# Layer 0 of a four-layer graph network on one core: reciprocal degrees spread through memory, and degrees moved forward in two engines' orders

## The reference, cut to what matters

```python
H = (adj != 0);  w = adj.reshape(N, -1)[:, :C]        # first row of adj: edge weights
Dn = 1 / einsum('nce,ne->nc', H, w)                   # reciprocal degree of a node (0 where not positive)
Be = 1 / H.sum(axis=1)                                # reciprocal count of an edge
conv(x) = Dn * H @ (Be * (H^T @ (x @ W^T))) + b
h = layer_norm(relu(conv(x, W1, b1)));  y = conv(h, W2, b2) + x
x = layer_norm(x + y)
```

## Time and profile before

| | us |
|---|---|
| median of three runs | 668.26 (666.8 to 669.39) |
| the profiled execution | 670.04 |
| its span | 668.2 |
| TensorE busy | 623.1 (93%) |
| VectorE busy | 560.8 (84%) |
| ScalarE busy | 526.6 (79%) |
| GpSimd busy | 376.5 (56%) |

### The profile page before, as it was taken

One profiled execution on the slowest core, in us unless ns is written; L12 is line 12 of the kernel. 1 busy time (PEld: TensorE's weight loads), 2 busy tenths in 40 slices (PEclk: granted clock), 3 DMA queues, 4 the chain that ended last, 5 costly groups with the idle time before them and its releaser, 6 DMA issues.

```text
span 668.2 us, 15857 instructions
## 1 busy us (share of the span) xinstructions
PE 623.1 (93%) x5014; PEld 452.0 (68%) x5014; DVE 560.8 (84%) x1712; ACT 526.6 (79%) x1191; POOL 376.5 (56%) x448
## 2 busy tenths in 40 slices
PE   5989999999999999898999979999999997999993
PEld 4667777777777776565666646666666664778882
DVE  3889998888888888778999888988988987688886
ACT  4667888877777777868999788787877785899995
POOL 1234556665555557756777435353535353899983
PEclk9999999999999999998999999999999998999998
DMA  9591338354646433344655334545453443487773
GB/s 271 182 233 48 80 65 221 79 145 82 149 87 150 86 65 63 63 81 89 103 110 98 63 75 85 111 81 109 83 110 83 103 87 64 81 188 188 180 188 127
DMA packets 174466, 76.14 MB, mean 114 GB/s; under 512 B 122160, under 2 KB 173872, under 8 KB 174384
## 3 DMA queue, kind: packets, MB, share of 16 engines
q1 hardware_dynamic: 164208, 66.34, 42.3%
q0 software_dynamic: 8448, 8.39, 8.5%
q10 hardware_dynamic: 1728, 0.40, 0.3%
HBM read 28.97 MB, written 8.39 MB: 56 GB/s over the span
## 4 chain that ended last, share of the span: by engine, by line
PE 30%; DVE 8%; POOL 6%; DMA 6%; ACT 3%; issue 2%; SPq 0%; ACTq 0%; POOLq 0%; DVEq 0%
PE banks L86 9%; PE banks L88 8%; PE banks L87 8%; DMA xT_lo<-x_halves 3%; DMA l_TT_lo<-l_T_lo 3%; DVE l_st L1057 2%; POOL x_halves L1143 2%; POOL l_rstd L1082 2%; PE banks L1237 2%; POOL l_U L2048 1%; PE banks L1605 1%; POOL l_T_lo L1845 1%; ACT l_t L1658 1%; DVE l_u L1762 1%; DVE l_rsum L1768 1%
## 5 line engine op out<-in xcount | busy, mean ns | idle before, releaser
L1091 ACT ACTIVATE x_resident<-l_pre,l_nmr,l_rstd 128x256 f32<-128x256 f32 x256 | 140.8, 605 | 7.7 <-POOL l_nmr L1085 7.7
L983 POOL TENSOR_TENSOR hq<-hq 128x512 f32<-128x512 f32 x48 | 71.7, 1493 | 90.9 <-ACT hq L690 88.6
L1143 POOL TENSOR_TENSOR x_halves<-x_resident,x_halves 128x1024 f16<-128x1024 f32 x46 | 98.1, 2133 | 16.5 <-DVE l_pre L1339 9.9
L1057 DVE BATCH_NORM_STATS2 l_st<-l_pre 128x6 f32<-128x256 f32 x256 | 93.3, 410 | 0.0
L86 PE MATMUL banks<-Wk_lo,xT_hi 128*128 128x512 f16 (+1 forms) x256 | 83.4, 326 | 3.3 <-DVE l_pre L1339 1.8
L87 PE MATMUL banks<-Wk_hi,xT_lo 128*128 128x512 f16 (+1 forms) x256 | 83.3, 325 | 0.0
L88 PE MATMUL banks<-Wk_hi,xT_hi 128*128 128x512 f16 (+1 forms) x256 | 83.2, 325 | 0.0
L1082 POOL TENSOR_TENSOR l_rstd<-l_veps,minus_half 128x4 f32<-128x4 f32 x64 | 71.7, 1121 | 15.1 <-DVE l_veps L1071 11.2
L86 PE MATMUL banks<-W2T_lo,h_hi 128*128 128x257 f16 x256 | 70.2, 274 | 3.5 <-DVE h_lo L849 1.3
L88 PE MATMUL banks<-W2T_hi,h_hi 128*128 128x257 f16 x256 | 70.1, 274 | 0.0
L87 PE MATMUL banks<-W2T_hi,h_lo 128*128 128x257 f16 x256 | 70.1, 274 | 0.0
(11 more groups left out here) (200 smaller groups left out, 1904.8 us busy)
## 6 DMA issues: line engine op xcount, KB each, us to landing
adj<-in_adj SPq DMA_DIRECT2D x32, 256.0 KB, 3.5
x_halves<-in_x SPq DMA_DIRECT2D x16, 512.0 KB, 4.3
x_resident<-b_half SPq DMA_DIRECT2D x8, 1024.0 KB, 7.9
x_resident<-in_x POOLq DMA_DIRECT2D x16, 512.0 KB, 5.9
out<-x_resident SPq DMA_DIRECT2D x15, 512.0 KB, 3.2
x_resident<-in_L_gnn_W SPq DMA_DIRECT2D x2, 512.0 KB, 5.5
x_resident<-in_L_gnn_Wk SPq DMA_DIRECT2D x1, 768.0 KB, 9.6
xT_hi<-x_halves SPq DMA_TRANSPOSE x48, 3.2
```

The lines of the kernel that those rows point to most:

```text
L983: pool.tensor_tensor(hq[:, 0, :], hq[:, 0, :], hq[:, h, :], ALU.add).then_inc(hqs_ok, 1)
L1057: dve.bn_stats(L.st[p][:, j, :], L.pre[p][:, j, :]).then_inc(L.st_ok, 1)
L1091: act.activation(K.x[:, gcols(g, j)], L.pre[p][:, j, :], ACT.Identity, bias=L.nmr[p][:, j:j + 1], scale=L.rstd[p][:, j:j + 1]).then_inc(L. ...
L1143: pool.tensor_tensor(F.xs[p][1], x_group(K, g), F.xs[p][0], ALU.subtract).then_inc(F.x_lo, 1)
```

## The change

For groups 6 to 15 (`BY_ROWS = 6`) the spreading by TensorE and the copy by ScalarE are left out. SyncE writes `dinv` to a row of 2 KB in memory, waits until it has landed, and reads the row back, broadcast to 128 partitions, into `dbc`; the elements lie there in the order (node, graph), so `operator` reads `dbc` with a step of four. These two DMAs stand at the head of SyncE's step g, ahead of the loads of group g + 2. VectorE's two casts go, and `degrees` of the next group waits until the write has landed. For all groups from 2 on, TensorE's `degree` stands right behind `mix_x` and not behind `project(g-1, 2)`, and VectorE's `degrees` stands ahead of both `mixed_low`.

```diff
+BY_ROWS = 6
+        K.rows = nc.dram_tensor("degree_rows", (G, N, GP), F32)
@@ sync
+        def spread_degrees(g):
+            sp.wait_ge(dchain, upto(g, 4, 4))
+            sp.dma_start(K.rows[g], dinv[:]).then_inc(row_out, 16)
+            sp.wait_ge(row_out, 16 * (g - BY_ROWS) + 16)
+            sp.wait_ge(pf_ok, upto(g - 1, 1, 1))
+            sp.dma_start(dbc[:], K.rows[g:g + 1].rearrange("a n j -> a (n j)").to_broadcast([128, C])).then_inc(
+                dbc_in, 16)
@@ sync step
+            if has(0) and g >= BY_ROWS:
+                spread_degrees(g)
             if has(2):
                 load(g + 2, p)
@@ tensor: transpose_adj
-            if reused(g, 1):
+            if g > BY_ROWS:
+                pe.wait_ge(dchain, upto(g - 1, 4, 2))
+            elif g > 0:
                 pe.wait_ge(dbc_sb, upto(g - 1, 1, 1))
@@ tensor step
-            if has(0):
+            if has(0) and g < BY_ROWS:
                 spread_degrees(g, p)
...
                 mix_x(g, p, 1)
+            if has(1) and g > 0:
+                degree(g + 1, q)
             once(g, 0, W.fold, pe)
             if has(-1):
                 project(g - 1, 2)
-            if has(1):
+            if has(1) and g <= 0:
                 degree(g + 1, q)
@@ scalar step
-            if has(1):
+            if has(1) and g < BY_ROWS - 1:
                 copy_degrees(g + 1)
@@ vector: degrees
+            if g > BY_ROWS:
+                dve.wait_ge(row_out, 16 * (g - BY_ROWS))
             dve.tensor_tensor(dinv[:], drc[:], dpos[:], ALU.mult).then_inc(dchain, 1)
+            if g >= BY_ROWS:
+                return
@@ vector: operator
+            if g >= BY_ROWS:
+                dve.wait_ge(dbc_in, 16 * (g - BY_ROWS) + 16)
+                dve.tensor_tensor(pf[p][:].rearrange("p (j n) -> p j n", j=GP),
+                                  b_gram[:].rearrange("p (j n) -> p j n", j=GP),
+                                  dbc[:].rearrange("p (n j) -> p j n", j=GP), ALU.mult).then_inc(pf_ok, 1)
+                return
@@ vector step
+            if has(2) and g >= 0:
+                degrees(g + 2)
             if has(1):
                 mixed_low(g + 1, q, 0)
...
-            if has(2):
+            if has(2) and g < 0:
                 degrees(g + 2)
```

More of the change, by code:

```diff
@@ L475, in layer0 @@
         sem, ("adjT_ps", "adjT_sb", "inc_ok", "wcol_ok", "small", "incb_ok"))
-    deg_ps, gram_ps, dinv_ok, dbc_ps, dbc_sb, pf_ok = map(
-        sem, ("deg_ps", "gram_ps", "dinv_ok", "dbc_ps", "dbc_sb", "pf_ok"))
+    deg_ps, gram_ps, dinv_ok, dbc_ps, dbc_sb, pf_ok, row_out, dbc_in = map(
+        sem, ("deg_ps", "gram_ps", "dinv_ok", "dbc_ps", "dbc_sb", "pf_ok", "row_out", "dbc_in"))
     px_ps, px_hi, px_lo = map(sem, ("px_ps", "px_hi", "px_lo"))
@@ L486, in layer0 @@
     K.hid_read = h_hi, hf_ok
-    K.first_x, K.first_free = L.x_new, dict(adj=adjT_ps, inc=gram_ps, degree=deg_ps, spread=dbc_sb, operator=pf_ok,
+    K.first_x, K.first_free = L.x_new, dict(adj=adjT_ps, inc=gram_ps, degree=deg_ps, spread=dchain, operator=pf_ok,
                                             relu=(h_hi, hf_ok), z=zf_ok, zvar=zvar_ok, squares=sq_lo, wk=W.wk_lo, out=L.pre_ok, copied=adjT_sb)
@@ L853, in operator @@
             dve.wait_ge(gram_ps, upto(g, 1, 1))
-            dve.wait_ge(dbc_sb, upto(g, 1, 1))
             if reused(g):
                 dve.wait_ge(y_ps, upto(g - 2, 2, 2))
+            if g >= BY_ROWS:
[4 more added lines that the diff above has]
+                return
+            dve.wait_ge(dbc_sb, upto(g, 1, 1))
             dve.tensor_tensor(pf[p][:], b_gram[:], dbc[:], ALU.mult).then_inc(pf_ok, 1)
@@ L1211, in project @@
             elif j < 2:
-                pe.wait_ge((free["spread"], free["operator"])[j], G)
+                pe.wait_ge((free["spread"], free["operator"])[j], (4 * G, G)[j])
             else:
```

## The result

The changed kernel takes 676.12 us (median of 4 runs, 675.45 to 685.58), the kernel before in the same comparison 668.70 (666.8 to 669.39): a ratio of 1.0144, 95% interval 1.0082 to 1.0206. It is slower. The profiled execution took 675.45 us, its span is 673.6, 5.4 us more than before.

What follows compares the result with a forecast made beforehand. TensorE was taken to bound layer 0 (busy 15.93 of 16.08 us a period). -3.0 (groups 6 to 15) + 3.3 (early steps) + 0.3 (behind fills) + 4.5 (group 6) = +5.1 us on 668.26, giving 673.4; range 665.5 to 679.

Steps and rivals of the forecast that it cites:

- What goes: Groups 6 to 15 without spreading and copy: 0.3 us gained a group, between 0.1 and 0.5; -3.0 us in ten groups.
- The bank wait: TensorE's third block of hidden products waits for ScalarE's reads of the first: 0.23 us newly lost where spreading goes.
- the hole: TensorE idle 0.28 us behind the degree products, waiting for ScalarE's copy of z; can close once the copy dbc goes.
- the block by hqs_lo: GpSimd's hqs_lo may hold VectorE's degree product at its new place; first low half then some 0.6 us late.
- Steps 1 to 5: Degrees ahead of late low halves of x: +0.95 at steps 2 and 4, +0.45 at 1 and 3, +0.5 at 5; +3.3 us.
- the port: A VectorE operation with two SBUF inputs stands still while GpSimd works; l_mdiff, 0.15 us elsewhere, took 0.96.
- Behind a fill: Groups 8, 10, 12: the degrees' write queues behind a 1 MB fill of x; +0.1 us each, +0.3 together.
- my lower bound: Earliest landing of the write behind a fill: with the fill, 7.5 us after T, the end of the mixing of x.
- Group 6: Its write stands behind two fills, dbc at 120.6; TensorE gets the edge weights 4.5 us late, bounds +3.5 and +6.
- the write isn't held back: Rival, chance 0.22: the 2 KB pass the fills, group 6's dbc is there by 114; 668 us.
- the early steps don't pay: Rival, chance 0.12: VectorE's late start in steps 1 to 4 is made up, the hole closes too; 664.5 us.
- GpSimd wins the port against h_lo: Rival, chance 0.12: GpSimd's first sum of squares starts first, h_lo waits 1.2 us; 0.7 us lost a group, 683 us.

Runs made afterwards that it cites:

- experiment 5: The change with the memory way only from group 7 on and the old degree orders up to there; ratio 0.9971 to the kernel before.
- experiment 1: The change with the memory way only from group 7 on, group 6 spread by TensorE again; ratio 1.0033 to the kernel before.
- experiment 3: The change with the two new orders alone, all 16 groups spread by TensorE and copied by ScalarE; ratio 1.0150 to the kernel before.
- experiment 4: The change with both DMAs of the degrees issued behind the load of x, ahead of that step's fill; ratio 1.0023 to the kernel before.
- experiments 6 and 9: Transposes of next adj between second and third hidden blocks: 6 on experiment 5, ratio 0.9992; 9 also with all degrees in their old place, 0.9967.

## Why the prediction was right, and where it was off

The direction and the order of size came out: +5.1 us predicted, 673.4 us; the profiled executions differ by 5.4, the medians by 7.4. That 5.4 lies so near 5.1 is in part luck. T1 to T15 grew by 6.69, and the start of this execution, which the change doesn't touch, was 0.94 us shorter (T1 at 34.99 against 35.93). The experiments split T1 to T15 in three parts that add up to its +6.69. Since two of them aren't independent, the last column has the same part from the other pair of kernels:

| part | predicted | measured | from | other pair |
|---|---|---|---|---|
| memory way, groups 7 to 15 | -2.7 + 0.3 = -2.4 | -2.94 | experiment 5 less before | |
| new order in steps 1 to 5 | +3.3 | +4.16 | experiment 1 less experiment 5 | +2.99 |
| group 6 through memory | +4.5 - 0.3 = +4.2 | +5.47 | change less experiment 1 | +6.64 |

**What goes.** Right, and a little too low: 0.40 us a group where I took 0.3, between the two ends that I had worked out. The bank wait of the earlier trace rows came as described (198.10 - 197.23 = 0.87 between two starts 0.65 apart: 0.22), the hole closed, and the block by hqs_lo was there (0.36 us). What decided was that TensorE's low halves came in all the same, late by no more than about a tenth; I had left that open.

**Steps 1 to 5.** The mechanism was right in steps 1 to 4, the size 0.8 too low: 3.60 where I took 2.8. Steps 2 and 4, read from rows, came out at 0.95 and 0.94. Steps 1 and 3, which I put at 0.45 each, cost 0.76 and 0.95. At step 3 the term left out what I used elsewhere, the port: the product took 0.43 us (72.96), beside an hqs_lo of 72.22 to 73.37; and VectorE stood idle for 0.29 us in front of the second low half (75.18), for which the trace names no engine. At step 2 TensorE waits 1.29 us for the edge weights at the degree products, which I had allowed for only in the steady period. It sets nothing there: the second low half ends at 58.84 and the hidden products begin at 58.90, so it is the low halves that cost the 0.95, as I had it. Step 5 is the step that was wrong. I had its product blocked by hqs_lo, +0.5; in the change it took 0.16 us and the step cost nothing. The loss of 0.70 is there only where group 6 keeps its casts (experiment 1), and it is a cast that is blocked. The sentence that six operations cost nothing in a steady step was wrong too: experiment 3 has 0.59 us a period.

**Behind a fill.** I took +0.1 for each of the groups 8, 10 and 12. In the change there is none: the write lands 0.1 to 0.2 us behind the fill, as my lower bound had it (T + 7.5), and dbc is there 0.1 to 0.4 us ahead of the operator. The write took 5.1 to 5.9 us there and not about 7, because SyncE came to it only at T + 2.0 to T + 2.5, behind the issue of the fill; the landing is the same. That is thin. In experiment 5 the operator of group 8 waited 0.52 us for dbc and TensorE 0.39 for the edge weights. At group 6 the write came when it was predicted: 117.1, shifted by the 2.7 us that the fill starts later (109.87 against the earlier trace rows), is 119.8; it was 119.3.

**Group 6.** Two terms were mis-sized. The read took 5.3 us, not 3.5. GpSimd's 512 KB onto x (issued 117.56) and adj (119.76) ran beside it, and the DMA engines' mean busy share was 0.99; in experiment 4, which issued it 3.1 us earlier, it took 3.5 at a share of 0.64, though a fill was issued right behind it. So the cause of the 5.3 is argued, not isolated. And TensorE's clock fell during the idle time, for which my sum had no term: 1.5 us in the mixing, 0.6 at the degree products behind it. Against these, 1.0 us and not 0.23 of the operator's lateness was covered (6.68 on VectorE, 5.65 on TensorE). TensorE's first wait was for the operator itself, at the mixing, and not for the edge weights behind it, by which I had counted.

**The rivals.** That the write isn't held back: 8.0 us at group 6 rule it out. That the early steps don't pay: they paid 3.60 in steps 1 to 4. That GpSimd wins the port against h_lo: it was the other way round. h_lo kept its 0.70 us in the table of groups, and GpSimd's first sum stretched from 1.32 us to 1.65 to 1.80 in the change.

## What to carry to other kernels

A DMA is priced by what its queue holds in front of it: 2 KB behind 1 MB land with the 1 MB. An order that looks free in one period has to be checked against the steps where an engine carries extra work, and against what another engine does at the new place: here 0.16 us became up to 0.92. And a stall of several microseconds on TensorE can cost more than its length: 5.65 us of idle time slowed the next sixteen products by 1.5 us. When one wait on TensorE is filled, look which chain ends last next, before counting it as gained.

## What the runs showed that I had not expected

- TensorE's clock: behind 5.65 us of idle the granted clock was 0.57 for 3.5 us and 16 matmuls took 3.47 us instead of 1.95; behind 5.44 us 0.50 and 3.76; behind 0.72 us 1.00 and 2.02. Of the 1.5 us, 0.6 reached the end, since TensorE would have waited for the edge weights anyway.
- A write of 2 KB to memory landed 1.4 us after its issue at best, 4.5 and 5.1 behind one fill issued 2.5 and 1.8 us before it, and 8.0 behind two fills. In the change, the groups without a fill took 2.4 to 4.3. Issued while a fill was under way, it landed 0.1 to 0.3 us behind the fill in every run; behind a load of x it mostly did the same, and at times came up to 1.7 us behind it.
- GpSimd's hqs_lo held up not only the product with two inputs but a cast of four elements per partition with one: 1.06 us instead of 0.17 (experiment 1).
- Moving 0.22 us of work into one wait of TensorE (experiments 6 and 9) moved the wait twice and gained nothing.
